# Last experts of a four-layer kernel: the first four tiles started beside the last attention batch, and the opening written out in order up to tile nine

## The reference, cut to what matters

```python
xn = layernorm(x)
normed = layernorm(xn, ln1_g, ln1_b)
blended = ls1 * ((1 - alpha) * ssm(normed) + alpha * gated_attention(normed))   # 16 heads of 8, 8 batches of 256
h = layernorm(xn + blended, ln2_g, ln2_b)
probs = softmax(h @ Wg); topp, topi = top_k(probs, 2)                            # "mix" router, 8 experts
moe  = sum over the two experts of topp_e * ((silu(h @ W1[e]) * (h @ W3[e])) @ W2[e])
s = ...xn, blended, ls2 * moe, weighted by the halting weights...
# the other part, "FFN": its own router and 8 other experts
t = rmsnorm(xn); logits = t @ gate_w + gate_b; top 2, softmax
ffn = xn + sum over the two experts of p_e * (swiglu(t @ w1[e] + b1[e]) @ w2[e] + b2[e])
x = x + s * silu(ffn)
```

## Time and profile before

| | |
|---|---|
| median of 3 runs | 916.22 us (911.16 to 916.53) |
| profiled execution, its own time | 915.85 us |
| span of the profile | 914.3 us |
| busy in the span | PE 694.1 (76%), DVE 588.8 (64%), ACT 395.7 (43%), POOL 286.8 (31%) |
| mean granted TensorE clock | 0.858 |
| attention ends (L2982, batch 7) | 707.16 us from the start of the span |
| first send of `sent2` | 747.70 us |
| mix tile 39 is turned | 813.46 us |

### The profile page before, as it was taken

The page is one execution under the profiler, slowest core; times in us unless marked ns, Lnnn a source line. Parts: engine busy times, 40 slices in busy tenths (PEclk is TensorE's granted clock), DMA queues, the critical chain, the costliest instruction groups (busy, mean ns, idle before and its releaser), DMA issues. The chain is left out here.

```text
span 914.3 us, 14444 instructions
## 1 busy us (share of the span) xinstructions
PE 694.1 (76%) x4255; PEld 520.0 (57%) x4255; DVE 588.8 (64%) x1609; ACT 395.7 (43%) x974; POOL 286.8 (31%) x303
## 2 busy tenths in 40 slices
PE   4889958671588829904996779899997879979891
PEld 2889844671477727703885547556564535546561
DVE  4566549545859841158567655688993478964794
ACT  3200234441664414304444433567776435537670
POOL 1353116342000037410100000236452037777762
PEclk9989969765689969956999779899999569989996
DMA  9992001211000032034600932122221013322515
GB/s 287 243 273 91 1 1 47 56 52 53 28 20 1 0 19 40 19 97 166 266 1 9 196 102 64 27 70 76 80 63 26 9 33 83 79 75 72 171 56 144
DMA packets 79563, 72.97 MB, mean 80 GB/s; under 512 B 9617, under 2 KB 73884, under 8 KB 78976
## 3 DMA queue, kind: packets, MB, share of 16 engines
q1 hardware_dynamic: 68000, 57.56, 23.4%
q0 software_dynamic: 7072, 12.40, 5.2%
q10 hardware_dynamic: 4416, 2.10, 0.9%
HBM read 42.85 MB, written 27.46 MB: 77 GB/s over the span
## 5 line engine op out<-in xcount | busy, mean ns | idle before, releaser
L3408 POOL DMA_INDIRECT ys<-work,back_to x78 | 79.4, 1018 | 72.0 <-DVE work L3378 42.5
L2503 DVE TENSOR_REDUCE work<-banks 128x2 f32<-128x512 f32 x128 | 83.2, 682 | 14.3 <-PE banks L2494 13.6
L3309 PE MATMUL banks<-weights,work 128*128 x156 | 87.9, 648 | 0.0
L2494 PE MATMUL banks<-work 96*128 96x256 bf16 x256 | 50.4, 282 | 9.1 <-DVE work L2503 4.1
L3290 PEld LDWEIGHTS banks<-consts,work 128*128 128x128 f32 x156 | 18.9, 147 | 64.5 <-DVE work L3368 34.3
L816 POOL DMA_INDIRECT xs<-t,idx x48 | 49.6, 1033 | 15.3 <-issue 11.9
L1196 POOL DMA_INDIRECT g<-rows,back_to x16 | 15.3, 958 | 123.3 <-DVE back_to L1914 118.7
L3301 PE MATMUL banks<-weights,work 128*128 x312 | 53.3, 296 | 0.2
L2907 PE MATMUL banks<-work 99*128 99x256 bf16 x256 | 49.4, 280 | 1.4 <-issue 1.3
L3301 PEld LDWEIGHTS banks<-weights,work 128*128 128x128 f32 x312 | 43.1, 200 | 2.6 <-issue 1.0
L885 PE MATMUL banks<-consts,g 128*128 128x128 f32 x32 | 7.4, 425 | 45.9 <-DVE g L417 45.9
(11 more groups left out here) (503 smaller groups left out, 1964.4 us busy)
## 6 DMA issues: line engine op xcount, KB each, us to landing
weights<-in_w SPq DMA_DIRECT2D x1, 6668.0 KB, 19.5
weights<-in_w SPq DMA_DIRECT2D x1, 4569.5 KB, 33.5
work<-xs SPq DMA_DIRECT2D x62, 64.5 KB, 1.8
weights<-in_r SPq DMA_DIRECT2D x1, 2950.5 KB, 26.1
xs<-zero SPq DMA_DIRECT2D x1, 2600.0 KB, 26.7
xs<-zero SPq DMA_DIRECT2D x1, 2580.0 KB, 33.3
work<-xs SPq DMA_DIRECT2D x39, 65.0 KB, 1.9
weights<-in_w SPq DMA_DIRECT2D x1, 2124.5 KB, 12.2
```

The source lines that it names most:

```text
L2494: ins = pe.matmul(ps[:, r * NS:(r + 1) * NS], q[0:self.ROWS, h * NS + r * 128:h * NS + r * 128 + 128], k[0:self.ROWS, h * NS:(h + 1) * NS] ...
L2503: v.tensor_reduce(self.mxb[:, 2 * h:2 * h + 2], self.n.bank(bank).rearrange("p (r n) -> p r n", r=2), AX, ALU.max, negate=True).then_inc(* ...
L3309: pe.matmul(self.mid(t), self.hT[t % 4], w1[:, bass.ds(off[t] * 4, 512)], start=True, stop=True).then_inc(*self.prod1.up())
L3408: g.indirect_dma_start(ys[:, :], bass.IndirectOffsetOnAxis(ap=n.back_to[:, t:t + 1], axis=0), self.yb[t % self.RETURNS], None, bounds_chec ...
```

## The change

- The first four tiles are begun inside the attention's last batch. On PE, turn(0) to turn(3) stand at the end of the attention's steps 116, 119, 122 and 125, in bank 0; first(0), (1), (2) at the end of steps 128, 132 and 134. On DVE the copies with the gain (now a `tensor_scalar` in `dve_turned`, instead of ACT's L3323) stand in steps 117, 120, 123 and 126, and sum(0), sum(1) in steps 130 and 133.
- SP's loads of the rows are where they were: behind SP's whole part of the attention.
- After the attention PE does turn(4), first(3), turn(5), first(4), turn(6), first(5), turn(7); then only turning and logits, in banks 0 and 2 in turn; then first(6), first(7) and the router's prefix sums; then middle and second of the first tiles. first(t) for t from 4 to 7 waits for `lin` (DVE's last clip of tile t-4) instead of `aT`; in return middle(m) for m below 4 waits for `lin` of tile m+4, because both use one bank.
- On DVE sum(2), sum(3), then logits and top 2, a(0) to a(3), then sum(4), sum(5), sum(6), y(0), y(1), sum(7) between the router's steps. On ACT tiles 4 and 5 are copied before the norm's square root, and silu(0) to silu(3) come after all turning.
- The loop starts at tile 8 on every engine, one round per tile. FfnGate's `idle` is FFN + 7 = 46.
- The buffers are placed anew, so that `hm` lies where batch 6 of the attention had been.

```diff
--- before.py
+++ after.py
@@ HeadsSoftmax.pe / HeadsSoftmax.dve, end of each step s
+            self.experts.beside_pe(s)
+            self.experts.beside_dve(s)
@@ LastExperts
-    ALONE = 11
+    EARLY, LOOP, ALONE = 4, 8, 11
...
-            cut(*x) for x in ((0, C + 2, 8), (1040, C), (1552, 512), (3600, 512), (5648, 256), (6672, C, self.RETURNS)))
+        self.rows, self.hT, self.ha, self.hm, self.at_, self.yb = (
+            cut(*x) for x in ((0, C + 2, 8), (1040, C), (1552, 512), (4096, 512), (6144, 256, 3), (6912, C, self.RETURNS)))
+        self.at_ += cut(3600, 256, 1)
...
-        return self.n.bank(0 if t >= self.ALONE and (t - self.ALONE) % 2 == 0 else 2, 128)
+        return self.n.bank(0 if t < self.EARLY or t >= self.ALONE and (t - self.ALONE) % 2 == 0 else 2, 128)
...
-        return self.n.bank(3 + t % 4)
+        return self.n.bank((4, 3, 6, 5)[t % 4])
...
+    def pe_turn(self, t):
...
+        if t == 0:
+            pe.wait_ge(*n.heads.mx.at(126))
+            pe.wait_ge(*n.heads.mx.at(127))
+        else:
+            pe.wait_ge(*self.xT_done(self.bank_user(t)))
+        if t == self.ALONE:
+            pe.wait_ge(*self.mix.placed.at(1))
+        pe.wait_ge(*self.row_in[t % 8].at(t // 8))
+        pe.transpose(self.turn_bank(t), self.rows[t % 8][:, 0:C], self.c["ident"]).then_inc(*self.turned.up())
+    def pe_first(self, t):
...
+        pe.wait_ge(*self.xT_done(t))
+        if t < 3:
+            pe.wait_ge(*(n.heads.exp.at(125), n.heads.exp.at(127), n.heads.oT.at(14))[t])
+        elif t >= self.LOOP:
+            pe.wait_ge(*self.aT.at(t - 4))
+        elif t >= 4:
+            pe.wait_ge(*self.lin.at(t - 4))
+        pe.matmul(self.mid(t), self.hT[t % 4], w1[:, bass.ds(off * 4, 512)], start=True, stop=True).then_inc(*self.prod1.up())
+    def pe_middle(self, m):
...
+        pe.wait_ge(*self.a.at(m))
+        if m < 4:
+            pe.wait_ge(*self.lin.at(m + 4))
...
+    def beside_pe(self, s):
+        if s in (116, 119, 122, 125):
+            self.pe_turn((s - 116) // 3)
+        if s in (128, 132, 134):
+            self.pe_first((128, 132, 134).index(s))
+    def beside_dve(self, s):
+        if s in (117, 120, 123, 126):
+            self.dve_turned((s - 117) // 3)
+        if s in (130, 133):
+            self.dve_sum((130, 133).index(s))
@@ Opening.pe
+        e.pe_turn(4)
+        e.pe_first(3)
+        e.pe_turn(5)
+        e.pe_first(4)
+        e.pe_turn(6)
+        e.pe_first(5)
+        e.pe_turn(7)
+        take(t)
+        self.tensor.wait_ge(*e.xT_done(7))
+        take(t)
         take(r)
         take(t)
         take(r)
-        take(e, 2)
         take(t)
         take(r, 2)
-        take(e, 4)
+        e.pe_first(6)
+        e.pe_first(7)
         take(r)
-        yield from self.rest(e)
+        e.pe_middle(0)
+        e.pe_middle(1)
+        e.pe_second(0)
+        e.pe_turn(8)
+        e.pe_middle(2)
+        e.pe_second(1)
+        e.pe_middle(3)
+        e.pe_second(2)
+        e.pe_turn(9)
+        e.pe_second(3)
+        e.pe_middle(4)
+        e.pe_turn(10)
+        yield from e.pe_rest()
@@ Opening.dve
-        take(e, 9)
-        take(r, 2)
-        take(e, 2)
-        take(r, 2)
-        take(e)
-        take(r, 3)
-        take(e)
-        yield from self.rest(e)
+        e.dve_sum(2)
+        e.dve_sum(3)
+        take(r, 2)
+        for k in range(4):
+            e.dve_a(k)
+        e.dve_sum(4)
+        take(r)
+        e.dve_sum(5)
+        take(r)
+        e.dve_sum(6)
+        e.dve_y(0)
+        take(r)
+        e.dve_y(1)
+        e.dve_sum(7)
+        take(r, 2)
+        e.dve_a(4)
+        e.dve_y(2)
+        e.dve_a(5)
+        e.dve_y(3)
+        yield from e.dve_rest()
@@ layer3
-    n.turn = Turn(..., banks=(0, 0, 0, 0))
+    n.turn = Turn(..., banks=(0, 2, 0, 2))
-    gate = FfnGate(n, ffn_rows, ffn_got, experts.FFN + 10)
+    gate = FfnGate(n, ffn_rows, ffn_got, experts.FFN + 7)
```

More of the change, by code:

```diff
@@ new lines, in act_aT, with act_rest @@
+    def act_aT(self, m):
+        a = self.scalar
+        if m >= self.TILES:
+            return
+        if m >= 4:
+            a.wait_ge(*self.prod2.at(m - 4))
+        a.wait_ge(*self.a_turned.at(m))
+        a.activation(self.at_[m % 4], self.mid(m)[:, 0:256], ACT.Copy).then_inc(*self.aT.up())
+    def act_rest(self):
+        for t in range(self.LOOP, self.TILES + 4):
+            self.act_aT(t - 3)
+            self.act_turned(t + self.AHEAD)
+            self.act_silu(t)
+            yield
@@ new lines, in dve_a @@
+    def dve_a(self, m):
+        v, u = self.vector, m % 4
+        if m >= self.TILES:
+            return
+        if m >= 4:
+            v.wait_ge(*self.a_turned.at(m - 4))
+        v.wait_ge(*self.silu.at(m))
+        if self.ffn(m):
+            v.wait_ge(*self.lin.at(m))
+            v.scalar_tensor_tensor(out=self.ha[u][:, 0:256], in0=self.hm[u][:, 256:512], scalar=1.0, in1=self.ha[u][:, 256:512],
+                                   op0=ALU.add, op1=ALU.mult).then_inc(*self.a.up())
+        else:
+            v.tensor_tensor(self.ha[u][:, 0:256], self.hm[u][:, 0:256], self.mid(m)[:, 256:512], ALU.mult).then_inc(*self.a.up())
@@ L3418, in __init__, with begin @@
         super().__init__(n)
-    def rest(self, lane):
-        for _ in lane:
-            next(lane, None)
-            yield
+    def begin(self, eng):
+        for s in self.experts.after:
+            eng.wait_ge(*s)
     def pe(self):
-        e, t, r = self.experts.pe(), self.turn.pe(), self.route.pe()
-        take(e, 5)
-        take(t, 2)
+        e, t, r = self.experts, self.turn.pe(), self.route.pe()
+        self.begin(self.tensor)
+        e.pe_turn(4)
[8 more added lines that the diff above has]
+        take(t)
         take(r)
@@ L3580, in layer3 @@
     softmax.blend = blend
+    mix = Route3(n)
+    sent2 = Dispatch(n, "2", n.t1_ids, n.xs[2], 0, 2, [n.cleared[2].at(0), mix.placed.at(1)], ids=n.t1_ids[:, :, C], gates=n.routes[0][1])
+    experts = LastExperts(n, [n.heads.pass2.at(111), sent3.done()], route, mix, sent2, [n.heads.out.at(7)])
+    softmax.experts = experts
     n.run(softmax)
@@ L3583, in layer3 @@
     norm = BlendNorm(n, n.s, n.t1, lambda t: [blend.done(t)])
-    n.turn = Turn(n, n.t1, lambda q: n.tT[:, q * 512:(q + 1) * 512], norm.done, n.w3["ln2_g"], n.w3["ln2_b"], banks=(0, 0, 0, 0))
-    mix = Route3(n)
-    sent2 = Dispatch(n, "2", n.t1_ids, n.xs[2], 0, 2, [n.cleared[2].at(0), mix.placed.at(1)], ids=n.t1_ids[:, :, C], gates=n.routes[0][1])
-    experts = LastExperts(n, [n.heads.pass2.at(111), sent3.done()], route, mix, sent2, [n.heads.out.at(7)])
+    n.turn = Turn(n, n.t1, lambda q: n.tT[:, q * 512:(q + 1) * 512], norm.done, n.w3["ln2_g"], n.w3["ln2_b"], banks=(0, 2, 0, 2))
     xt = n.xT[:, :, :].rearrange("p b n -> p (b n)")[:, 0:NT * C]
```

269 lines of the change are left out of this document (128 added, 141 removed).

## The result

| | before | changed |
|---|---|---|
| median | 915.10 us (908.39 to 920.97, 19 runs) | 920.65 us (916.42 to 928.91, 19 runs) |
| ratio to before | 1 | 1.0077, 95% [1.0048, 1.0105] |
| profiled execution, own time / span | 915.85 / 914.3 us | 917.93 / 916.4 us |
| mean granted clock | 0.858 | 0.868 |

Slower by 0.8%, where no difference was forecast (915.2 us). To find the place, the span is cut at points that both programs have. The anchor at the front is the group of four transposes that stands just ahead of head 116's scores.

A forecast was written before the change was run, and what follows sets the result against it. No single engine bound it; the last send's landing and the row load behind it set tile 39's start. +3.7 +1.3 +0.6 -7.9 +1.6 = -0.7 on 915.85 gave 915.2 us, range 907.0 to 922.0.

The forecast's parts named there:

- (a): In the attention's last batch, PE's turn(0) waits for its row: +3.7 us, bounds 1.9 and 3.7.
- (b): In the attention, the clock falls after turn(0)'s wait: +1.3 us, bounds 0 and 3.4.
- (c): Four turns, three firsts inside the attention's last batch: +0.6 us, bounds 0.2 and 2.4.
- (d): Attention's end to the router's first step on DVE: 14.1 us instead of 26.6.
- (e): Router's first step to the first send: 18.5 us instead of 13.9; both opening stretches together 7.9 us less.
- The rival that the opening stays at the lower clock: Turning and logits after the attention run slower, opening gains 2.0 instead of 7.9: 922.9 us, chance 0.16.
- The rigid 65.8 us: First send to tile 39 takes 65.8 us whatever PE and DVE do; PE idle over 10 us before it.
- (f): Tiles 0 to 7 through DVE some 15 us earlier: worth nothing, and the loop's own order is the same.
- (g): The gate's first step on DVE comes a tile early and waits longer: +1.6 us, bounds 0 and 3.3.
- the three rivals: Wait at turn(0) hidden, 908.2 us (0.18); opening at lower clock, 922.9 (0.16); router's gain not reaching POOL, 923.1 (0.06).
- The second: The rival with the opening after the attention staying at the lower clock: 922.9 us, chance 0.16.

The follow-up runs named there:

- e1: The changed kernel with PE's read of the tile's expert number moved back to the head of each loop step; 924.01 us, ratio 1.0101.
- e4: The changed kernel with turns 0 to 3 beside heads 119, 121, 123, 125 and DVE's copies one head behind each; 922.84 us, ratio 1.0068.
- g3: The kernel before with its gate on DVE one tile earlier, on ACT unchanged; 963.27 us on a slow chip, ratio 1.0078.
- j3: The kernel before with only the ends' gate two tiles later on DVE and ACT; 913.18 us, medians differ by 2.3 us.
- g4: e4 with the gate as in g1; 960.17 us on a slow chip, ratio 1.0047.
- j2: The same kernel as g4, on a chip where before takes about 915 us; 915.12 us, ratio 0.9989.
- k1: e4 with the gate three tiles later on DVE and ACT, its last silu two tiles earlier on ACT; 961.45 us on a slow chip, ratio 1.0006.
- e2: The kernel before with PE's read of the expert's number moved to right before the first; 921.88 us, ratio 1.004.
- e3: e1 with the gate one tile later on both engines (FFN + 8); 921.16 us, ratio 1.0076.
- j1: The same kernel as g1, on a chip where before takes about 915 us; 917.65 us, ratio 1.0025.
- g1: The changed kernel with only the gate moved, one tile later on DVE and one earlier on ACT; 965.9 us on a slow chip, ratio 1.0104.
- h2: The same kernel as g1, beside the changed kernel on another slow chip; 5.7 us under the changed kernel by the medians.
- h3: The same kernel as g4, beside h2 on a slow chip; another 4.8 us less than h2 by the medians.
- j4: j2 with first(0) to first(2) at the head of PE's opening and sums 0 and 1 behind DVE's norm; 931.27 us, ratio 1.0122.

## Why the prediction was wrong

By its steps:

- *(a) Turn(0) waits for its row*: right. 2.04 us, released by the row's DMA, inside the bounds 1.9 and 3.7 but at the other end from the 3.7 I took. The other seven profiles with turn(0) at head 116 show 2.1 to 2.7. SP issued its loads at 690.38 and the turn began 2.1 us later; the Trainium skill (DMA: Bandwidth & Descriptors, section "Anatomy of one DMA") gives 2.0 of fixed cost for transfers that GpSimd issues, and this one, which is SP's, is close to it. The single 3.7 of the earlier trace rows was the wrong one to take.
- *(b) The clock after it*: right in kind, not in every execution. In the changed kernel's profile it stayed at 1.00 and the attention took 18.6 us; in e1, with a wait of 2.10, the window behind it was granted 0.67 and the attention took 20.0:

```profile
696.00:700.00 4.00, 4.00 (x31) 2.83 (x32) 0.39 (x2) 2.06 (x4) 0.00 (x0) 0.67 0.38 102
```

  The 1.3 us forecast are the 1.4 between the two. Of the profiles with turn(0) at head 116, five have 20.0 to 20.6 and three 18.6 to 18.7.
- *(c) Turns and firsts in the attention*: 0.6 forecast, 1.1 measured (e4's 16.4 against 15.3), 0.75 of it the firsts. Both repeat where the granted clock of this stretch is 1.00: 15.3 in before, g3 and j3, 16.4 in e4, g4, j2 and k1. A fallen clock does as much: e2, whose attention is unchanged, took 16.6 at 0.84.
- *(d), (e) The opening*: right in form, 1.5 us short: 13.95 for 14.1 to the router's step; 34.08 for 32.6 to the first send, and 32.6 to 35.9 in the profiles of e1, e3, e4, j1 and j2. A gain of 4.7 to 8.0 us, with the forecast's 7.9 at its good end. How much is gained goes with the clock up to L651: 35.5 to 35.9 us where it is 0.76 to 0.78 (e1, e3, e4), 34.0 to 34.1 at 0.87 (changed, j1), 32.6 at 1.00 (j2). The rival that the opening stays at the lower clock fell (0.87).
- *The rigid 65.8 us*: the number came (65.85), the reason only in part. PE was to stand more than 10 us before tile 39; it stood there not at all, since its loop had become 0.27 us a tile slower and it arrived with the rows. With the read early (e1) it stands 7.8 us. e2, e4, j1 and j2 have 67.6 to 68.0 instead: e2 because PE itself comes late, the other three because the row of tile 39 does, for which PE waits 0.6 to 1.6 us.
- *(f) "The loop's own order is the same"*: false in two places, the number's read on PE and, far worse, the gate's rounds against the loop's.
- *(g) "The gate comes a tile early", +1.6*: **this is the step that failed.** It cost 7.5 us. I counted DVE's rounds to the gate's first step, and there the wait grew as said, by 1.3; the upper bound of 3.3 even holds the 3.0 measured with the clock. But I counted neither ACT's rounds nor the gate's later steps. Of its last silu, which moved a tile later on ACT while DVE's product moved a tile earlier, there is no word in the working, and it cost 4.6. Mending both counts (j1) brings back 5.3 of the 7.5; the 2.1 left are about what the late read costs behind tile 39 in e2 (2.0), a term that (f) put at nothing.

With the forecast's other terms (+5.6, -7.9) and 7.5 in place of 1.6 the sum is 921.1, close to the median of 920.65. The profile's own are +3.3, -6.5, +0.1, +7.5. That the median difference (5.6 us, or 7.0 by the ratio) is over these 4.4 fits the executions with a fallen clock and with 67.6 to 68 in the rigid stretch, 1.4 and about 2 us more; no run took them apart.

None of the three rivals named the cause. The second came nearest in time, 922.9, for a reason that the profile shows not to hold.

## What to carry to other kernels

When one pass is woven round by round with another, a change of where its loop begins moves every later step of the other, and on each engine by its own amount: count the rounds on all engines, and at the last shared step as well as at the first. A wait added between two engines that both feed TensorE costs its own length and then a stretch at the lower clock (1.3 and 1.7 us here at the gate's first step). An edit that starts a chain earlier pays only as far as nothing behind it was nearly as late: here PE's loop, lengthened by a read that had been hidden, had used up the 4.9 us that it stood waiting before, and in e2 came 2.2 us late.

## What the hardware showed that I had not expected

The same wait doesn't always cost the clock. PE stood 2.86 us in the kernel before and in j1, for the same operation; in the one the first behind it took 1.02 us, in the other 2.07. What goes with it is the place of the read. Of the kernels whose PE stood 2.5 to 3.0 us there, the two with the read at the head of the step (before 2.86, e3 3.01) kept the clock, and all six with the read right before the first (e2 2.92, g1 2.60, h2 2.53, h3 2.60, j1 2.86, j4 3.02) lost it; e2 differs from before in nothing else (one profile each). It isn't the whole story: behind DVE's wait for the gate's last silu PE stood 2.84 us in e1 and in e3, both with the early read, and the clock stayed in e1 (first 1.02 us) and fell in e3 (1.92).

On three of the five chips the kernel before took 959 to 963 us instead of 915. There the experts' loop stops for up to 9 us at several of the tiles 13 to 28, on PE, DVE and ACT at about the same time, and what the engines wait for isn't in the records. From the timeline of g3, a kernel that differs from before in the gate alone:

```profile
793.16 0.29 DVE L3378 SCALAR_TENSOR_TENSOR work<-banks,weights 128x128 f32<-128x128 f32 x1 [6.51 <-remote]
...
795.81 0.42 ACT L3347 ACTIVATE work<-work 128x256 f32<-128x256 f32 x1 [5.81 <-issue]
...
796.30 0.69 PE L3290 MATMUL banks<-consts,work 128*128 128x128 f32 x2 [6.09 <-issue]
```

First send to turn 39 takes 98 to 103.5 us there instead of 65.8. What these stops are stays open. So does the best kernel: on the chips at 915 none beat before by more than j3's 2.3 us, and the early read, the later turns and the later gate weren't tried together.
